# A transformer block on one core: x is normalised on ScalarE, half of the turned weight chunks are copied there, and the scale of the weights is found in one trip over TensorE

## What is computed

```python
x = x + _L0_attn_ref(_layernorm(x, axis=-1), L0_attn_Wqkv, L0_attn_Wo)
x = x + _L0_ffn_ref(_layernorm(x, axis=-1), L0_ffn_w1, L0_ffn_w3, L0_ffn_w2)
# attention: 16 heads of 32, causal softmax, output times Wo
# network: out = (silu(x @ w1q.T) * (x @ w3q.T)) @ w2q.T, hidden size 1365
def ternary_quant(w):
    s = jnp.mean(jnp.abs(w))
    q = jnp.clip(jnp.round(w / s), -1.0, 1.0) * s
    return w + jax.lax.stop_gradient(q - w)
```

## Time and profile before

| | us |
|---|---|
| median of 3 runs | 602.69 (601.48 to 603.0) |
| the profiled execution | 603.58, of which the span from first to last instruction is 601.8 |
| PE busy | 562.4 |
| DVE, POOL, ACT busy | 392.2, 282.5, 255.3 |

### The profile page before, as it was taken

The page is one execution under the profiler, slowest core; times in us unless marked ns, Lnnn a source line. Parts: engine busy times, 40 slices in busy tenths (PEclk is TensorE's granted clock), DMA queues, the critical chain, the costliest instruction groups (busy, mean ns, idle before and its releaser), DMA issues. The chain is left out here.

```text
span 601.8 us, 9390 instructions
## 1 busy us (share of the span) xinstructions
PE 562.4 (93%) x3395; PEld 271.2 (45%) x3395; DVE 392.2 (65%) x986; ACT 255.3 (42%) x428; POOL 282.5 (47%) x332
## 2 busy tenths in 40 slices
PE   1599779899999999999999999999999999999997
PEld 1245435344554444444455444444454444444443
DVE  7978788978599676654577667553487754363331
ACT  1558659745445264422144354523035653013320
POOL 6005297587451837470163546731606679112320
PEclk9999988999999999999999999999999999999999
DMA  8668438233015202102510210312500001100001
GB/s 332 202 209 229 117 123 231 99 89 106 1 37 158 71 19 54 35 19 71 139 54 1 79 29 19 89 37 80 148 19 2 1 2 41 66 17 19 0 19 52
DMA packets 36098, 46.88 MB, mean 78 GB/s; under 512 B 4650, under 2 KB 25130, under 8 KB 36052
## 3 DMA queue, kind: packets, MB, share of 16 engines
q1 hardware_dynamic: 36052, 46.28, 25.1%
HBM read 33.55 MB, written 12.58 MB: 77 GB/s over the span
## 5 line engine op out<-in xcount | busy, mean ns | idle before, releaser
L1012 PE MATMUL work<-late,w_ternary 128*128 128x512 f16 (+1 forms) x704 | 160.5, 379 | 2.4 <-DVE late L832 1.5
L857 DVE CUSTOM_DVE_ANT_0 masked<-score_bank,mask 128x512 f16<-128x512 f32 (+3 forms) x256 | 111.8, 486 | 43.8 <-PE score_bank L1083 43.2
L672 ACT ACTIVATE early<-prob_bank,scalars 128x512 f32<-128x512 f32 x160 | 100.8, 684 | 83.1 <-PE prob_bank L1105 82.7
L1012 PEld LDWEIGHTS work<-late,w_ternary 128*128 128x128 f16 (+1 forms) x704 | 68.9, 100 | 77.7 <-DVE o_sb L876 2.5
L571 POOL TENSOR_SCALAR_AFFINE_SELECT early<-early 128x640 f32<-128x640 f32 (+2 forms) x96 | 43.5, 484 | 80.1 <-ACT early L672 80.1
L1174 PE MATMUL work<-w_ternary,late 128*128 128x512 f16 (+1 forms) x352 | 78.0, 379 | 0.0
L597 POOL TENSOR_TENSOR late<-late 128x512 f16<-128x512 f32 (+1 forms) x44 | 50.6, 1156 | 46.7 <-ACT late L692 46.6
L893 DVE SCALAR_TENSOR_TENSOR late<-late,work 128x512 f32<-128x512 f32 (+1 forms) x44 | 30.1, 684 | 46.0 <-ACT late L685 46.0
L580 POOL TENSOR_TENSOR early<-early 128x768 f32<-128x768 f32 x32 | 58.0, 1814 | 2.1
L1105 PE MATMUL prob_bank<-q_stack,k_stack 98*128 98x512 f16 (+3 forms) x256 | 51.0, 303 | 4.5 <-ACT early L672 2.1
L1174 PEld LDWEIGHTS work<-w_ternary,late 128*128 128x128 f16 (+1 forms) x352 | 34.2, 98 | 40.4 <-issue 0.6
(11 more groups left out here) (119 smaller groups left out, 816.0 us busy)
## 6 DMA issues: line engine op xcount, KB each, us to landing
xn<-in_L_attn_x SPq DMA_DIRECT2D x16, 256.0 KB, 3.3
q_stack<-q_hi_spill SPq DMA_DIRECT2D x32, 128.0 KB, 2.9
k_stack<-k_hi_spill SPq DMA_DIRECT2D x32, 128.0 KB, 3.1
x_res<-in_L_attn_x SPq DMA_DIRECT2D x12, 256.0 KB, 2.8
out_y<-x_res SPq DMA_DIRECT2D x12, 256.0 KB, 2.0
late<-in_L_ffn_w SPq DMA_DIRECT2D x4, 682.5 KB, 4.5
early<-in_L_ffn_w SPq DMA_DIRECT2D x3, 768.0 KB, 12.4
late<-in_L_ffn_w SPq DMA_DIRECT2D x3, 768.0 KB, 5.8
```

The lines of the kernel that those rows point to most:

```text
L672: act.activation(probs[:, u, :], prob_bank[u % 2][:], ACT.Exp, scale=scalar(exp_scale)).then_inc(prob_free, 1)
L857: dve.tensor_tensor_reduce(masked[:, k % 2, 0:n], score_bank[u % 2][:, off:off + n], mask[:, S - n:S], 1.0, LOWEST, ALU.add, ALU.max, row_ ...
L1012: last = pe.matmul(bank, lhs, rhs, start=(n == 0), stop=(n == len(terms) - 1))
```

## The change

1. `norm_x` moves from DVE to ACT, as one activation with scale rstd and bias -mean * rstd. The bias is a new small instruction on POOL behind each `power` of x.
2. `top_turn` is now one product: DVE multiplies the identity by the column of maxima (`on_diagonal`), PE multiplies a matrix of ones by that, so that every partition gets the whole row, and DVE reduces it on all partitions, scales and inverts. `top_spread` is gone.
3. ACT copies the turned weight chunks with odd numbers (15 of the 33), DVE the others.
4. The fill of the three `k_stack` tiles becomes a step of its own (`unit`). The first stands ahead of the statistics in POOL's list, the other two among the roundings of w1.
5. All five lists are new. A branch for `sums` without additions on POOL is there too, but `ADDING = 0` leaves it unused.

```diff
+                if n == "x":
+                    pool.wait_ge(rstd_done[n], ST * b + i + 1)
+                    pool.tensor_scalar(shift[:, i:i + 1], mean_var[n][:, i, 0:1], rstd[n][:, i:i + 1], -1.0,
+                                       ALU.mult, ALU.mult).then_inc(shift_done, 1)
...
-                for t in k_stack:
-                    pool.memset(t[:], MAX_UNIT).then_inc(unit_rows_set, 1)
+
+            def unit_rows(i):
+                pool.memset(k_stack[i][:], MAX_UNIT).then_inc(unit_rows_set, 1)
...
+            def norm_x(b, i):
+                act.wait_ge(shift_done, ST * b + i + 1)
+                act.activation(xn[:, i, :], xn[:, i, :], ACT.Identity, bias=shift[:, i:i + 1],
+                               scale=rstd["x"][:, i:i + 1]).then_inc(norm_done["x"], 1)
...
+            def weight_turn(step):
+                _, m, c = step
+                bank, cols = bank_of(step), P if c < HC - 1 else HLAST
+                src = work[bank][:, 0:256].bitcast(F16).rearrange("p (k c) -> p k c", k=KC)
+                full(act, step)
+                if m == "w2":
+                    dst = t_down[0:cols, c, :].rearrange("p (k c) -> p k c", k=KC)
+                    act.activation(dst, src[0:cols, :, :], ACT.Copy).then_inc(work_free[bank], 1)
+                else:
+                    act.activation(t_up[m][:, :, c * P:c * P + cols], src[:, :, 0:cols],
+                                   ACT.Copy).then_inc(work_free[bank], 1)
...
+            def on_diagonal(n):
+
+                if n == 0:
+                    dve.wait_ge(ident_made, 1)
+                dve.wait_ge(rows_found, n + 1)
+                dve.tensor_scalar(diagonal[n], ident[:], scalar(top_rows + n), None, ALU.mult).then_inc(diagonal_made, 1)
...
             def top_turn(step):
 
                 bank, n = bank_of(step), TOPS.index(step[1])
                 full(dve, step)
-                dve.tensor_reduce(scalars[0:1, top:top + 1], work[bank][0:1, 0:P], AX_X, ALU.max).then_inc(top_found, 1)
+                dve.tensor_reduce(scalar(top + n), work[bank][:, 0:P], AX_X, ALU.max).then_inc(work_free[bank], 1)
+                emptied(dve, step)
+                dve.tensor_scalar(scalar(tops + n), scalar(top + n), 1e-30, 1.0 / WEIGHT_TOP,
+                                  ALU.max, ALU.mult).then_inc(top_found, 1)
                 dve.wait_ge(top_found, n + 1)
...
             def top_turn(step):
-                bank = open_work(step)
-                n = TOPS.index(step[1])
-                pe.wait_ge(top_rows_done, n + 1)
-                pe.transpose(work[bank][0:1, 0:P], scalar(top_rows + n), ident[:]).then_inc(work_full[bank], 1)
-
-            def top_spread(step):
 
                 bank = open_work(step)
                 pe.wait_ge(consts_done, 1)
-                emptied(pe, ("top_turn", step[1]))
-                pe.matmul(work[bank][:, 0:1], ones[0:1, :], scalars[0:1, top:top + 1],
+                pe.wait_ge(diagonal_made, TOPS.index(step[1]) + 1)
+                pe.matmul(work[bank][:, 0:P], ones[:], diagonal[TOPS.index(step[1])],
                           start=True, stop=True).then_inc(work_full[bank], 1)
```

Of the lists, a line of PE's stands for the rest. Line by line:

```diff
-        xt:0,0-2 top_turn:qk top_spread:qk xt:0,3 top_turn:v top_spread:v q:0 k:0 q:1 top_turn:wo k:1 v:0,0-1
+        xt:0,0-3 top_turn:qk top_turn:v q:0 k:0 q:1 v:0,0 top_turn:wo k:1 weight_mean:w1 v:0,1 scores:0,0 q:2
```

More of the change, by code:

```diff
@@ new lines @@
+        top_turn:v split:1-3 split:8 q:0 stats_x:1,0 k:0 wo_max q:1 top_turn:wo stats_x:1,1 weight_mean:w1
+        split:4 stats_x:1,2 split:5-6 k:1 scores:0,0 split:7 scores:0,1 q:2 stats_x:1,3 weight_turn:w1,0
+        scores:0,2 k:2 weight_turn:w1,2 scores:0,3 q:3 scores:0,4 weight_turn:w1,4 max_row:0 weight_turn:w1,6
+        scores:1,0-1 wo_split weight_turn:w1,8 scores:1,2 pad:w3 scores:1,3 weight_turn:w1,10 scores:1,4 k:3
+        xt:1,0 max_row:1 scores:2,0 xt:1,1 scores:2,1-2 weight_mean:w3 xt:1,2-3 stats_x:2,0 scores:2,3
@@ L180 @@
+        gate:3,9 lin:3,9 gate:3,10 lin:3,10 down:3,0-3
     """,
     "pe": """
[L182 to L185 removed]
@@ new lines @@
+        scores:1,2 k:3 probs:0,1 scores:1,3 probs:0,2 xt:1,0 scores:1,4 probs:0,3 xt:1,1 max_row:1 probs:0,4
+        scores:2,0 xt:1,2 scores:2,1 xt:1,3 weight_mean:w3 scores:2,2 values:0 scores:2,3 sums:0 probs:1,0 q:4
+        probs:1,1 weight_turn:w3,0 scores:2,4 probs:1,2 weight_turn:w3,1 probs:1,3 weight_turn:w3,2 k:4
+        max_row:2 weight_turn:w3,3 scores:3,0 probs:1,4 weight_turn:w3,4 scores:3,1 weight_turn:w3,5-6
+        scores:3,2 q:5 weight_turn:w3,7 scores:3,3 values:1 sums:1 probs:2,0 scores:3,4 weight_turn:w3,8
@@ new lines @@
+        probs:2,1-2 k:5 probs:2,3 weight_mean:w2 max_row:3 weight_turn:w3,9 scores:4,0 weight_turn:w3,10
+        probs:2,4 q:6 weight_turn:w2,0 scores:4,1 values:2 weight_turn:w2,1 scores:4,2 sums:2 probs:3,0 k:6
+        probs:3,1 scores:4,3 probs:3,2 weight_turn:w2,2-3 scores:4,4 weight_turn:w2,4 probs:3,3 weight_turn:w2,5
+        max_row:4 probs:3,4 scores:5,0 q:7 scores:5,1 values:3 scores:5,2 sums:3 probs:4,0 scores:5,3 v:1,0-1
+        probs:4,1 scores:5,4 k:7 weight_turn:w2,6 project:0,0-1 weight_turn:w2,7 max_row:5 v:1,2
@@ L330, in build @@
         rstd = {n: sb(f"{n}_rstd", [P, ST], F32) for n in "xy"}
+        shift = sb("shift", [P, ST], F32)
+        diagonal = [yn[:, 0, n * P:(n + 1) * P] for n in range(len(TOPS))]
         RAW = HC * D
@@ L1131, in sums @@
                     pe.wait_ge(consts_done, 2)
-                pe.wait_ge(added_done, ADDS * (s + 1))
+                if s < ADDING:
+                    pe.wait_ge(selected, SELECTS * (s + 1))
+                    for kt in range(ST):
+                        for h in range(HG):
+                            u, off, n = place(h, kt)
+                            last = pe.matmul(work[bank][HD * h:HD * (h + 1), S - n:S], ones[:, 0:HD],
+                                             probs[:, u, off:off + n], start=(kt == 0), stop=(kt == ST - 1),
+                                             skip_group_check=True)
+                    last.then_inc(work_full[bank], 1)
+                    return
+                pe.wait_ge(added_done, ADDS * (s - ADDING + 1))
                 for cols in (slice(0, P), slice(P, S)):
```

312 lines of the change are left out of this document (147 added, 165 removed).

## The result

The changed kernel took 593.16 us (median of 4 runs, 592.5 to 593.71), the kernel before 602.85 on the same chip. The ratio is 0.9847, with a 95% interval of 0.983 to 0.9863. The medians differ by 9.7 us; the ratio, which is not the ratio of the medians, makes it 9.2 us. The prediction had 594.4 us, from 8.3 us less. The profiled execution took 592.5 us, with a span of 590.4 against 601.8.

A forecast was written before the change was run, and what follows sets the result against it. PE, busy 562.4 of 601.8 us, bounds the kernel; only its waits or slow stretches can shrink. Terms -5.9 - 1.9 - 1.0 + 0.5 = -8.3 from 603.58 give 595.3, or 594.4 us at the median; range 588 to 600.5.

The forecast's parts named there:

- The start, predicted -5.9: Up to the first product of q: it starts at 19.7 us instead of 25.64; bounds -6.7 to -3.6 us.
- the walk: DVE's new list at the start, stepped through with old durations: first split done, q starting at 19.7 us.
- The trip over PE: At the start, in the scale of the weights: a low half of 0.64 us hides the one trip.
- Is it kept?: Behind q's start: loads and Wo's maximum (30.2 us) just fit before PE's four steps end at 30.3 to 32.
- caught by the next limit: Rival at the start: w3's loads or Wo's scale come late, 2.5 to 6 us lost, about 599; chance 0.17.
- The low half of Wo, predicted -1.9: Near 80 us: moved up a slot, away from POOL's additions, so the last addition ends 1.9 us earlier.
- Row maxima, predicted -1.0: From 60 to 150 us: fewer DVE steps shorten PE's 4.4 us of waits by 1.0; bounds 0 and -3.4.
- ACT's load, predicted +0.5: About 90 to 100 us: five more turned chunks, Wo's high half gone; +0.5 us, bounds 0 and +3.
- the sign that the prediction called wrong: A wait of PE for ACT at weight_turn or for a free bank would show the forecast wrong; no size.
- The slower rival: ACT holds work banks for 15 turned chunks; at 1.0 us each 609 us, deciding from 0.55; chance 0.06.
- a new DVE–POOL pair of long instructions at 38 or 46 us: Where the moved k_stack fills now stand: a sign that would show the forecast wrong; no size.
- More given back (the clock): Rival: 2.5 us of slow-clock stretches and 3.4 us more of row-max waits also go, 588.5 us; chance 0.20.

The follow-up runs named there:

- the second execution: Second profiled execution of the unaltered changed kernel, from a later timing against the kernel before: ratio 0.9852, median 595.16 us; the execution's span was 594.3 us.

## Why the prediction was right, and where it was off

- **The whole: a good forecast, and some luck.** The sum of -8.3 us was made of waits of PE alone. PE's waits fell by 6.4 us, in both profiled executions of the changed kernel. The rest is busy time of PE, which the sum left out and only a rival had: 5.0 us less in the first execution, 1.1 in the second. So 594.4 lies close to 593.16 in part by luck: the waits fell by 1.9 us less than forecast, and busy time that the sum left out made up for it.
- **The start, predicted -5.9.** q came at 20.00 us, 5.64 earlier; the walk had 19.7, and it held step by step: reductions 1.2 each, low halves 0.68, small steps 0.15 to 0.3. What the walk left out is the load of the q and k columns: the first reduction waited for it for 0.33 us here and for 1.06 in the second execution. The first scores came 4.8 us earlier, so 0.8 was lost on the way, with no wait of PE between. The first products start 0.43 us apart and the later ones 0.22, and 13 of them were slow where 9 were before, which makes about 0.8 us; the trace has the granted clock at 1.00 over the slow and the fast ones alike, so why they are slow isn't shown. Of the parts that share this term, the fills are shown directly: put back, they hold the product with the identity for 1.64 us. What the move to ACT is worth at the start alone isn't separated from the chance in the load.
- **The trip over PE.** One low half was to hide it; it did but for 0.35 us of waiting.
- **Is it kept?** Yes, and for the reason given: the low half of k:0 was begun at 28.68 us and Wo's maximum began at 29.29, where I had 28 and, for its end, 30.2 (31.6 measured). The kernel with the fills alone shows what would have been otherwise: of 4.7 us at q only 2.3 reached the end. So "caught by the next limit" exists, and the new lists avoid it. Its first half, that w3's loads would start only some 3 us earlier, came true and more (42.66 us against 42.70), but no wait of PE for w3 is among the largest.
- **The low half of Wo, predicted -1.9.** Alone in the old kernel -2.05, undone in the new +2.6 (by the medians -1.5 and +1.6). Right in mechanism and, within what can be measured, in size.
- **Row maxima, predicted -1.0.** The two waits were 3.2 and 1.2 us and are 0.4 (line 1116) and 2.0 (line 1109), 2.0 less. Two waits for the DMA that places the low halves of the maxima ahead of probabilities, 2.0 us in all, are gone too. But new waits stand in the same stretch: some 3 us ahead of the turned chunks (lines 1229 and 1232, mostly for a bank that DVE's low half of q or k or an ACT step had to empty) and 1.4 ahead of a part of the scores, for which the trace names no cause. So little is left of this term in the whole. And the reason that I gave, fewer steps on DVE, isn't it (its 22 us off DVE also held the standstill of 4.7 us, which the start had already counted): with the normalisation back on DVE they are 0.4 and 2.6, with the turned chunks back 2.8 on line 1109. The order of the new lists must have done it; which part of the order wasn't tried.
- **ACT's load, predicted +0.5.** In the time it can't be told from nothing. ACT was busy for 271.6 us (275 predicted), and PE's wait for ACT ahead of the probabilities went from 2.1 to 1.6. But the sign that the prediction called wrong, PE waiting for ACT at a turned chunk, is there once, between 80 and 90 us, where ACT is busy for 10.00 of 10 us:

```profile
87.81 0.40 PE L1232 MATMUL work<-ident,late 128*128 128x128 f16 x4 [0.68 <-ACT w_ternary L694]
```

The second execution has no such wait over 0.2 us. The slower rival, ACT holding work banks, needed 0.55 us for each of 15 chunks, 8.3 us in all. Taking all of them off ACT moved the ratio by -0.0010; even between the far ends of the two intervals it is 0.0062, or 3.7 us, which is 0.25 a chunk.
- **What was mis-sized.** Taking the normalisation off DVE. The prediction doesn't split its start, but ahead of the run I gave this part 2.0 to 2.5 us there and 2 to 4 in all; undone, it cost 5.1 (4.1 by the medians). Of PE's waits in it 1.78 us come from the pair at 37.54 us, which the prediction named as a sign ("a new DVE–POOL pair of long instructions at 38 or 46 us") but did not price for the case that DVE keeps a step that can be held. In the changed kernel there is a small pair at that place, a rounding of 1.22 us instead of 0.69. The step itself took 0.81 us on ACT, where I had 0.72.
- **More given back (the clock).** In the first profiled execution the slow slices went, as this rival says, and PE's busy time fell by 5.0 us; in the second they came back, and it fell by 1.1. The time fell by only 0.9 us more than the sum (1.4 by the medians). Executions of the kernel before with a mean granted clock of 0.997 took 600.2 to 603.6 us, those with 0.989 to 0.992 took 602.2 to 606.2; of the changed kernel one at 0.988 took 593.08 and one at 1.0 took 593.71, and the profiled execution of its second timing, with 0.96 from 20 to 140 us, 596.38, against 592.5 for the first. So some 2 us may hang on the clock; how much of these is the clock and how much the waits that come with it stays open.

The parts, undone one at a time, sum to 5.1 + 2.9 + 2.6 + 1.2 - 0.6 = 11.2 us, more than the 8.9 of the whole. That would fit the fills and the normalisation, two cures for the same stop: each undone alone brings a part of it back. But the intervals of the five are wide enough to hold the difference too, and by the medians the parts sum to 6.6 us, less than the 8.4 of the whole. So nothing is shown by this sum.

## What to carry to other kernels

Look for pairs of long instructions on DVE and POOL that end together; moving one of them in a hand-written list was worth about 2 us in both cases here. A step that such a collision can stop may be worth moving to ACT where ACT has room, even if it takes longer there (0.81 us against 0.54). And an earlier start is kept only if everything behind it in the same list is ready earlier too: ask for each load and each scale who is queued behind the wait for it, on DVE and on PE.

## What was unexpected

- Fills on POOL, which only write, held a DVE product of 128x128 in f32 for 1.64 us (1.93 instead of 0.29), while reductions beside them kept their time; a rounding and a fill together held a normalisation of 128x512 for 2.2. In both cases DVE's instruction ended within 0.3 us of POOL's.
- POOL's rounding can be the one that waits: it took 1.22 us (0.69 alone) at 36.99 us, beside DVE's low half of a chunk of Wqkv, which started at 36.98 and kept its 0.75 us.
- A normalisation on ACT that takes both its scale and its bias from a column took 0.808 us, an ACT instruction of the same size with one column 0.72. I had used the latter.
- Moving q's start by 2.8 us moved the end by nothing that could be measured. PE then waited for DVE's low half for v and for Wo's scale instead.
